# DLRM tower on one core: SyncE fetches three fields of tile 14 row by row, and start and end are reordered

## The reference

```python
e = jnp.stack([tbl_0[ids[:, 0]], ..., tbl_31[ids[:, 31]]], axis=1)     # 2048 x 32 x 16
z = jnp.sum(e[:, row, :] * e[:, col, :], axis=2)                       # all pairs row < col: 2048 x 496
h = jnp.concatenate([z, dense_ctx], axis=1)                            # 2048 x 512
h = jnp.maximum(h @ W_top1 + b_top1, 0.0)
h = jnp.maximum(h @ W_top2 + b_top2, 0.0)
y = h @ W_top3
```

## Time and profile before

| | us |
|---|---|
| median of 3 runs (316.6 to 318.14) | 317.02 |
| time of the profiled execution | 318.14 |
| its span in the profile | 316.3 |
| outside of the span | 1.84 |
| PE busy / share | 271.7 / 86% |
| VectorE busy / share | 249.1 / 79% |
| GpSimd busy / share | 227.9 / 72% |
| granted clock of TensorE, mean | 0.984 |

### The profile page before, as it was taken

How to read it: one execution, slowest core, us unless ns; L and a number is a source line. 1 busy time by engine, 2 the same in 40 slices (tenths; PEclk the granted TensorE clock), 3 DMA queues, 4 the chain that set the end, 5 groups by cost and what they waited for, 6 DMA issues and landing times.

```text
span 316.3 us, 7362 instructions
## 1 busy us (share of the span) xinstructions
PE 271.7 (86%) x2721; PEld 259.0 (82%) x2721; DVE 249.1 (79%) x312; ACT 146.4 (46%) x311; POOL 227.9 (72%) x250
## 2 busy tenths in 40 slices
PE   0167969999999999999797998979799897994897
PEld 0167969999999999998787988979799797994795
DVE  7876999889898988794976769587685967849393
ACT  2896564636363646464343725425362541302322
POOL 6777777777777777777777777777777777777720
PEclk9999999999999999999999999999999998996999
DMA  7782021212031312121030301203030010010000
GB/s 163 201 278 85 7 72 19 78 9 78 9 77 9 71 14 64 23 54 32 6 78 7 78 7 14 71 7 78 6 77 8 6 8 7 7 9 6 6 5 2
DMA packets 19037, 14.51 MB, mean 46 GB/s; under 512 B 9728, under 2 KB 16462, under 8 KB 19023
## 3 DMA queue, kind: packets, MB, share of 16 engines
q1 hardware_dynamic: 10284, 11.69, 12.0%
q0 software_dynamic: 7680, 1.98, 8.1%
q10 hardware_dynamic: 1058, 0.66, 0.7%
HBM read 14.24 MB, written 0.08 MB: 45 GB/s over the span
## 4 chain that ended last, share of the span: by engine, by line
POOL 66%; issue 22%; PE 7%; DMA 2%; DVE 2%; ACT 1%; ACTq 0%
POOL emb L359 66%; PE bank L638 2%; PE bank L667 2%; DMA emb<-tbl,idx 1%; PE bank L749 1%; PE bank L658 1%; DVE prod L472 1%; DMA idx<-ids 1%; PE bank L773 1%; PE bank L674 0%; DVE emb L453 0%; ACT h2T L863 0%; ACT zT L852 0%; DVE z_last L500 0%; ACT y L869 0%
## 5 line engine op out<-in xcount | busy, mean ns | idle before, releaser
L359 POOL DMA_INDIRECT emb<-tbl,idx x240 | 226.7, 945 | 73.9 <-issue 72.8
L472 DVE TENSOR_TENSOR prod<-emb,bank 128x1904 f32<-128x1904 f32 (+5 forms) x51 | 94.4, 1853 | 40.2 <-DMA emb<-tbl,idx 40.2
L638 PE MATMUL bank<-ident,prod 128*128 128x128 f32 x752 | 94.6, 279 | 1.8 <-ACT named_eight L804 1.8
L638 PEld LDWEIGHTS bank<-ident,prod 128*128 128x128 f32 x752 | 88.5, 195 | 2.2 <-ACT named_eight L804 2.0
L620 PE MATMUL bank<-parts,onehot 125*128 125x160 bf16 (+1 forms) x816 | 80.7, 233 | 0.0
L620 PEld LDWEIGHTS bank<-parts,onehot 125*128 125x128 bf16 x816 | 65.5, 101 | 0.4
L658 PE MATMUL bank<-zT,w_sb 128*128 128x128 f32 x480 | 64.5, 279 | 1.3 <-ACT zT L852 1.3
L658 PEld LDWEIGHTS bank<-zT,w_sb 128*128 128x128 f32 x480 | 59.1, 194 | 1.8 <-ACT zT L852 1.8
L453 DVE TENSOR_REDUCE emb<-bank 128x480 f32 (+5 forms) x96 | 52.9, 585 | 6.6 <-PE bank L620 6.4
L617 PE MATMUL bank<-far_ten,named_ten 100*128 100x160 bf16 x160 | 38.8, 243 | 19.2 <-DVE emb L453 15.6
L858 ACT ACTIVATE h1T<-bank,b_sb 128x128 f32<-128x128 f32 x60 | 21.7, 364 | 42.9 <-PE bank L658 42.9
(11 more groups left out here) (69 smaller groups left out, 125.1 us busy)
## 6 DMA issues: line engine op xcount, KB each, us to landing
gids<-small_ids_f SPq DMA_DIRECT2D x16, 544.0 KB, 4.0
emb<-tbl,idx POOLq DMA_INDIRECT x240, 2.3
w_sb<-w SPq DMA_DIRECT2D x1, 1024.0 KB, 6.8
w_sb<-w SPq DMA_DIRECT2D x1, 512.0 KB, 6.7
tab<-tbl SPq DMA_DIRECT2D x7, 56.0 KB
tab<-tbl SPq DMA_DIRECT2D x5, 70.0 KB
tab<-tbl ACTq DMA_DIRECT2D x5, 70.0 KB
z_last<-dense SPq DMA_DIRECT2D x16, 8.0 KB, 1.7
```

Source lines behind the costliest of these rows:

```text
L359: nc.gpsimd.indirect_dma_start(emb[:, t, at:at + D], None, tables[f], bass.IndirectOffsetOnAxis(ap=idx[:, t, f:f + 1], axis=0)).then_inc(d ...
L472: return nc.vector.tensor_tensor(prod[:, at * D:(at + n * a) * D].rearrange("p (j i d) -> p j i d", j=n, d=D), strided(emb_at(t, PLACES[g] ...
L638: mm = nc.tensor.matmul(bank[:, Z_BANK + place, c * P:(c + 1) * P], v[:, d, :], ident[:], start=(d == 0), stop=(d == D - 1), is_transpose= ...
```

## The change

GpSimd leaves out three of tile 14's gathers (fields 29, 30 and 31) and so makes 237. SyncE fetches these fields instead: for each of the 128 rows it loads the three ids from SBUF into its registers and issues three DMAs of 64 bytes, 384 in all. They are spread over the run, 11 rows ahead of tile 2's loads and 9 rows after those of each of 13 more iterations. VectorE waits for them before the product of group 1 of tile 14. The fields change places: group 1 is now 29, 30, 31, 15, 17, and group 2 is 26, 27, 28.

At the start VectorE makes the masks of tiles 0 to 3 alone; those of the other twelve come in window 0, and are turned there. The first tile's look-ups go to a bank of their own for each round, TensorE makes 12 products without use ahead of them (`wake`), and VectorE takes the maxima of tile 0 between its other steps. Orders of loads change.

At the end chunk 2 of the last tile is summed by TensorE, not by VectorE; the last tile's `sum_pairs` are two and not four, of 51 and 61 pairs; `sum_chunk` of tile 14's chunk 2 comes ahead of `layer2(13)`; and in every window ScalarE does `copy_y` ahead of `copy_small`.

```diff
 SMALL = [f for f in range(F) if VOCABS[f] == 1250] + [f for f in range(F) if VOCABS[f] == 1000]
-LARGE = [f for f in range(F) if f not in SMALL]
+
+FETCHED = [29, 30, 31]
+FETCHED_TILE = TILES - 2
+LARGE = [f for f in range(F) if f not in SMALL + FETCHED]
+LARGE[7:7] = FETCHED
...
-TURN_SUMS = 2
+TURN_SUMS = 3
 SUM_AT = TURN_SUMS * P
 N_SUMS = N_PAIRS - SUM_AT
+
+FETCHES = [11] + [9] * (FETCHED_TILE - 1)
...
-        CAND_BANK = 7
-        TURN_BANK = [(6, 7), (3, 4), (5, 1), (3, 4)]
+
+        CAND_BANK, CAND_COL = 3, 400
+        WAKE_BANK, WAKES = 5, 12
+        TURN_BANK = [(6, 7), (3, 4), (5, 3), (4, 5)]
...
             load_tables(sp, 0)
-            load_tables(sp, 2)
...
-            load_tables(sp, 4)
+            load_tables(sp, 2)
+            load_tables(sp, 4, 0, 2)
             sp.wait_ge(groups_stored, 16)
             load_gids(0)
+            load_tables(sp, 4, 2)
+            load_tables(sp, 5)
             load_gids(1)
-            load_tables(sp, 5)
             load_dense(0)
...
+            def fetch(k):
+
+                first = sum(FETCHES[:k])
+                for b in range(first, first + FETCHES[k]):
+                    _, rows = nc.values_load_multi_w_load_instructions(
+                        idx[b:b + 1, FETCHED_TILE, FETCHED[0]:FETCHED[0] + len(FETCHED)],
+                        engines=[mybir.EngineType.SP], min_val=0, max_val=VOCABS[FETCHED[0]] - 1,
+                        skip_runtime_bounds_check_because="an id is a row number of its table")
+                    for i, (f, row_of) in enumerate(zip(FETCHED, rows)):
+                        at = (PLACES[1] + i) * D
+                        sp.dma_start(emb[b:b + 1, FETCHED_TILE, at:at + D], tables[f][bass.ds(row_of, 1), :]
+                                     ).then_inc(fetched[i], 16)
+
+            sp.wait_ge(ids_loaded, 16)
+            sp.wait_ge(distance_made, stretches_done(1, len(STRETCHES) - 1))
+            load_gids(3)
+            fetch(0)
             for t in range(2, TILES):
-
-                if t + 1 < TILES:
-                    sp.wait_ge(distance_made, stretches_done(t - 1, len(STRETCHES) - 1))
-                    load_gids(t + 1)
                 sp.wait_ge(summed, chunks_done(t - 2, CHUNKS - 1))
                 load_dense(t)
+
+                if t + 2 < TILES:
+                    sp.wait_ge(distance_made, stretches_done(t, len(STRETCHES) - 1))
+                    load_gids(t + 2)
+                if t <= FETCHED_TILE:
+                    fetch(t - 1)
...
                         f = FIELDS[GROUP_AT[g] + i]
+                        if t == FETCHED_TILE and f in FETCHED:
+                            continue
...
+            candidates(0, TURNED, 0)
...
+                if before == 0:
+                    candidates(TURNED, TILES, 3)
...
+                if fetch:
+                    dve.wait_ge(landed[1][place], 16 * (lands * GROUPS[1] - len(FETCHED)))
+                    for field in fetched:
+                        dve.wait_ge(field, 16 * P)
+                else:
+                    dve.wait_ge(landed[1][place], lands * 16 * GROUPS[1])
                 group_with_before(t, 1, 0, GROUPS[1]).then_inc(made, 1)
...
-                sum_pairs(t, place, 3 * P, PAIR_AT[5])
+                sum_pairs(t, place, SUM_AT, PAIR_AT[5])
...
-                row1, row2 = GROUP_AT[1], GROUP_AT[2]
+                row2 = GROUP_AT[2]
                 dve.wait_ge(summed, chunks_done(t - 2, CHUNKS - 1))
-                piece(0).then_inc(last_made, 1)
-                dve.wait_ge(last_made, 1)
-                sum_pairs(t, place, SUM_AT, PAIR_AT[3] + 3 * row1)
+                piece(0)
                 piece(1).then_inc(made, 1)
-                dve.wait_ge(made, steps_done(t, GROUP1_STEP))
-                sum_pairs(t, place, PAIR_AT[3] + 3 * row1, 3 * P)
                 dve.wait_ge(e_copied, copies_done(t, 2))
                 circle(t, 1)
-                piece(2)
-                piece(3).then_inc(last_made, 1)
-                dve.wait_ge(last_made, 2)
-                sum_pairs(t, place, 3 * P, PAIR_AT[5] + 2 * row2)
+                piece(2).then_inc(last_made, 1)
+                dve.wait_ge(last_made, 1)
+                sum_pairs(t, place, SUM_AT, PAIR_AT[5] + row2)
+                piece(3)
                 piece(4)
                 last_group_inside(t).then_inc(last_made, 1)
-                dve.wait_ge(last_made, 3)
-                sum_pairs(t, place, PAIR_AT[5] + 2 * row2, N_PAIRS)
+                dve.wait_ge(last_made, 2)
+                sum_pairs(t, place, PAIR_AT[5] + row2, N_PAIRS)
...
+                third_part(r)
+                if r == 2:
                     onehot_of_first()
-                third_part(r)
-            for r in range(len(ROUNDS)):
-                pick(0, r)
+                if r > 2:
+                    pick(0, r - 3, look_bank=r - 3)
+            for r in range(len(ROUNDS) - 3, len(ROUNDS)):
+                pick(0, r, look_bank=r)
...
-            window(TILES - 2, 0, TILES // 2, before=2)
+            window(TILES - 2, 0, TILES // 2, before=2, fetch=True)
...
+            def wake():
+
+                for k in range(WAKES):
+                    mm = nc.tensor.matmul(bank[:, WAKE_BANK, :], ident_bf[:], far_ten[:, 0:512], start=True, stop=True)
+                mm.then_inc(awake, 1)
...
+
+                    pe.wait_ge(masks_made, 2 * n_masks)
+                    turn_masks(1)
...
+            wake()
...
-                if r > 1:
-                    pe.wait_ge(picked, r - 1)
-                look_up(0, 0, r)
-            turn_masks(1)
...
+            sum_chunk(t - 1, 0, 2, GROUP1_STEP)
             layer2(t - 2)
             layer3(t - 2)
-            sum_chunk(t - 1, 0, 2, GROUP1_STEP)
...
             pe.wait_ge(z_copied, t + 1)
-            pe.wait_ge(z_summed, sums_done(t, 1))
-            turn(1, 2)
             add_chunks((0, 1))
+            sum_chunk(t, 1, 2, GROUP1_STEP)
             layer3(t - 1)
             pe.wait_ge(z_copied, t + 2)
             add_chunks((2,))
-            pe.wait_ge(z_summed, sums_done(t, 3))
+            pe.wait_ge(z_summed, sums_done(t, 1))
...
+                if before > 1:
+                    copy_y(t - 2)
                 if look:
                     copy_small(t + 1)
-                if before > 1:
-                    copy_y(t - 2)
```

More of the change, by code:

```diff
@@ L208, in dlrm_tower @@
         landed = [[sem(f"landed{g}_{i}") for i in range(2)] for g in range(len(GROUPS))]
+        fetched = [sem(f"fetched{i}") for i in range(len(FETCHED))]
         last_landed = [sem(f"last_landed{i}") for i in range(len(LAST_PIECES))]
@@ L275, in dlrm_tower, with load_tables @@
         block = ctx.enter_context(nc.Block())
-        def load_tables(eng, r):
+        def load_tables(eng, r, skip=0, count=None):
             first, n = ROUNDS[r]
-            for i in range(first, first + n):
+            for i in range(first + skip, first + (count or n)):
                 rows = tables[SMALL[i]].rearrange("(p x) d -> p (x d)", x=CANDS[i])
@@ L406, in _, with candidates @@
             nc.vector.tensor_copy(groups_f16[:], groups_int[:]).then_inc(groups_steps, 1)
+            def candidates(first, end, steps):
+                tiles = slice(first, end)
+                nc.vector.tensor_scalar(tenth[:, tiles, :], idx[:, tiles, :], 6554, None, ALU.mult
+                                        ).then_inc(cand_steps, 1)
+                nc.vector.tensor_scalar(of_eight[:, tiles, :], idx[:, tiles, :], 7, None, ALU.bitwise_and)
+                dve.wait_ge(cand_steps, steps + 1)
+                nc.vector.tensor_scalar(tenth[:, tiles, :], tenth[:, tiles, :], 16, None, ALU.logical_shift_right
+                                        ).then_inc(cand_steps, 1)
+                dve.wait_ge(cand_steps, steps + 2)
+                nc.vector.scalar_tensor_tensor(out=of_ten[:, tiles, :], in0=tenth[:, tiles, :], scalar=-10.0,
+                                               in1=idx[:, tiles, :], op0=ALU.mult, op1=ALU.add
+                                               ).then_inc(cand_steps, 1)
+                dve.wait_ge(cand_steps, steps + 3)
+                for at0, fields, cand in ((0, SMALL[0:TENS], of_ten), (TENS, SMALL[TENS:S], of_eight)):
+                    for pos, f, count in runs_of(fields):
+                        at = (at0 + pos) * SLOTS
+                        c = cand[:, tiles, f:f + count]
+                        number = bank[:, CAND_BANK, CAND_COL:CAND_COL + SLOTS]
+                        nc.vector.tensor_tensor(
+                            mask[:, tiles, at:at + count * SLOTS].rearrange("p t (f c) -> p t f c", c=SLOTS),
+                            strided(c, [c.ap[1], c.ap[2], [0, SLOTS]]),
+                            strided(number, [[0, end - first], [0, count], [1, SLOTS]]), ALU.is_equal
+                        ).then_inc(masks_made, 1)
@@ L418, in masks @@
[L418 to L428, removed]
@@ L430, in _ @@
-            masks(0, SMALL[0:TENS], of_ten)
```

(25 more changed lines are left out.)

40 lines of the change are left out of this document (20 added, 20 removed).

## The result

The changed kernel takes 357.6 us (median, 357.45 to 358.67) beside 317.3 us for the one before (316.6 to 318.14). The ratio is 1.128, with a 95% interval from 1.125 to 1.132. So it is slower by 40 us, where 312.9 us was forecast. The profiled run took 357.75 us, with a span of 355.8.

The account below looks back on a forecast made before the run. GpSimd's gathers set the later pace, TensorE's backlog the end. The last turn moves from 309.89 to 304.6, so 318.14 - 5.3 = 312.8, forecast as 312.9, with start and SyncE at zero; range 311.0 to 319.0.

Parts of the forecast that it names:

- the price of a row on SyncE: SyncE's queue, tile 14's 128 rows: 1.6 us a row (1.1 to 3.35), under the affordable 1.89, so no cost.
- register load of three ids: SyncE, each fetched row: loading its ids into registers takes 0.5 us, bounds 0.05 to 1.7.
- three issues: SyncE, each fetched row: issuing its DMAs, priced like a single-partition store, 0.93 us, at most 1.35.
- register work for addresses: SyncE, each fetched row: three to six register operations of 0.05 us, taken as 0.15.
- this rival: SyncE too slow: over 1.89 us a row, each 0.1 us costs 12.8 at tile 14's group 1; 327 us; chance 0.23.
- The ids: SyncE's queue: ids of tile t + 2 are late for ScalarE only if SyncE falls over 8 us behind.
- Rival 3: Nothing gained: SyncE's extra DMAs slow each GpSimd gather by 17 ns, 4.0 us in all; 317 us; chance 0.08.
- The start: Masks, banks and maxima in window 0: zero effect, since some 12 us of cover lie behind it.
- The end: Last windows: TensorE reaches the last turn at 304.6, VectorE's sum at 303.4; turn 5.3 us earlier.
- rival 1: TensorE's end keeps a low clock after idling, one such step costs 2.0 us: 314.9 us; chance 0.11.
- an accident: Tile 14's group 1, late landing: about 1.6 of 4.1 us from gather start to use, hardly in the median run.
- the second rival: SyncE too slow: with 0.45 us a DMA, a row takes 2.0 us, 14 us late, 327 us; chance 0.23.

Follow-up runs that it names:

- experiment 7: The changed kernel with its 384 DMAs from fixed rows, without register loads or register work: 312.20 us, ratio 0.980 to the kernel before.
- experiment 3: The changed kernel with SyncE's 384 DMAs into a spare tile nobody reads and all 240 gathers on GpSimd: 347.06 us, ratio 1.089 to the kernel before.
- experiment 4: The changed kernel with the ids of tiles 4 to 15 issued by ScalarE, fetches kept: 350.48 us, ratio 1.102 to the kernel before.
- experiment 6: The changed kernel with tile 14's ids brought to one partition and 27 ids a register load: 312.49 us, ratio 0.984 to the kernel before.
- experiment 1: The changed kernel without fetches, all 240 gathers on GpSimd, changed start, field order and end kept: 315.28 us, ratio 0.990 to the kernel before.
- experiment 8: Without fetches, against the kernel before: changed end alone 315.53 us; changed start and field order 317.49 us; two moved orders alone 315.72 us.
- experiment 2: The changed kernel with SyncE fetching two fields a row instead of three, 238 gathers: 313.09 us, ratio 0.983 to the kernel before.
- experiment 5: The changed kernel with the fetched fields' ids brought to one partition and nine ids a register load: 312.99 us, ratio 0.983 to the kernel before.

## Why the prediction was wrong

**The step that failed is the price of a row on SyncE.** The prediction set what SyncE can afford, 1.89 us, took 1.6 and so chose the wrong side. Measured is 2.27. Term by term:

| term of the row | predicted | measured |
|---|---|---|
| register load of three ids | 0.5 (0.05 to 1.7) | 0.94 |
| three issues | 0.93 | 0.88 (experiment 7) |
| register work for addresses | 0.15 (0.15 to 0.3) | 0.2 for two operations a DMA, with gaps 0.45 (2.27 - 0.94 - 0.88) |
| a row | 1.6 | 2.27 |

The load is the term that decides: with 0.94 in the place of 0.5 alone, the sum is 2.0 and over the limit; with the register work alone put right it is 1.9, at the limit. The issue was right: the single-partition store was its row, and the 0.40 of the 13-row load was not. The load was taken for something near a register operation, "since it uses no queue", and that was a guess and not a reading. In the bounds 1.1 to 3.35 the limit of 1.89 lay low, and the text even named 0.8 us of load as the point from which the cover is gone. A term with no row, wide bounds and a nearby threshold should have moved the likeliest case or at least stretched the range; 0.23 for this rival looks too little.

**The rival's mechanism was right, with its arithmetic.** It said 12.8 us at the end for each 0.1 us of a row. (2.27 - 1.89) x 128 = 49 us behind 278.5 would be 327; the product ran at 325.15, as SyncE started 0.9 us earlier than assumed and the last row was used about 1.1 us after its issue, not 1.7. With 49 us it would have said 312.9 + 49 = 362; measured 357.6. Its price of 327 us was for a row of 2.0, and that row was made dear by the wrong term: 0.45 for an issue (measured 0.295), with the load left at 0.5.

**The ids.** The prediction saw them behind the fetches and said that they are late only if SyncE falls behind. That happened in 11 windows, and experiment 3 shows that with it alone 29 us are lost. It adds little to the sum since experiment 4, without it, is only 7 us faster.

**GpSimd** worked as predicted: 237 gathers 1.25 us apart, unhindered by SyncE's DMAs. Rival 3 fell, with experiment 7 as its test.

**The start** was put at zero, and measured at a ratio of 1.000 (0.996 to 1.003).

**The end** was predicted step by step and experiment 6 met it where the fetch fits: product of group 1 at 278.5 (278.52), chunk 2 of tile 14 at 284.6 (284.29), VectorE's last sum done at 303.4 (302.8), last turn at 304.6 (304.56), time 312.9 (312.49). In the changed kernel this gain is there too, but hidden: 24.3 us from product to turn instead of 26.7, with TensorE at a granted clock of 0.50 (3.68 us for 16 instructions) after 9.22 us of waiting. That is rival 1 in another place.

**A smaller wrong reading.** I took the landing at 283.23, 4.1 us after its gather's start, for an accident. The run with two orders has it at 283.01, after a gather that starts at 279.13 too, 3.9 us; experiment 1 has 281.88 - 279.25 = 2.6 us, and the other two kernels of experiment 8 have 2.9 (the end alone) and 3.5 (the start alone). So it comes and goes, and is not rare. What causes it was not found.

## What to carry to other kernels

Work moved to an engine that shows as idle has a price for each item on that engine's sequencer, and it must be set against the time that it has: here 242.5 us for 128 rows. Where the price has no row in the trace, solve for the value at which the verdict turns, and if that value lies inside the bounds, treat both sides as likely. A queue that works off items between other loads delays those too, and freeing one consumer of two (experiments 3 and 4) gives back little, 7 to 11 us of 40; making the item cheaper (experiments 2, 5 and 6) gives it all.

## What the runs showed of the hardware

A register load from SBUF on SyncE took 0.74, 0.94, 2.12 and 5.66 us (medians) for 2, 3, 9 and 27 registers: about 0.33 us and 0.2 for each register. All 14 loads that started at a multiple of 16 bytes of their tile were faster, 0.93 to 1.01 us for 9 registers and 2.24 to 2.28 for 27. A DMA with an address from registers costs its sequencer 0.41 to 0.42 us (27 in 11.02 and 11.34, experiment 6), one with a fixed address 0.295. The dense load of 128 rows took 0.33 with a gap of 0.05, so a single row is not dearer to issue than many rows, other than the second rival assumed. The 13-row load took 0.40; why was not found.

The Trainium skill, "Runtime: NRT & Kernel Launch", section "Instruction fetch mechanics", states about 200 ns for each register of a load from HBM; the slope here, from SBUF, is the same in most loads (from 3 to 27 registers (5.66 - 0.94) / 24 = 0.197 us), and a third of it in the 14 faster ones ((2.26 - 0.98) / 18 = 0.07). The 600 ns of the Trainium skill, "DMA: Bandwidth & Descriptors", section "Latency and other measured facts", of which the prediction spoke, lie under all of these values.
